# Slot list in bf16 digits, and the lower rows of six output tiles scaled on ScalarE and added by transfers

## The chip, the cores and the metric

One NeuronCore of a Trainium2 chip runs the whole program. The metric is the device time of one execution in microseconds (us). Five engines work beside each other and meet only at semaphores: TensorE (PE in the profile, its weight loads PEld), VectorE (DVE), ScalarE (ACT), GpSimd (POOL) and SyncE (SP, which here only starts transfers). Sixteen DMA engines carry what SP, ACT and POOL put into their queues.

## The reference

1024 tokens of 512 values each. A dense layer with a LoRA adapter for each sequence gives the input of a feed-forward part: a router picks 2 of 16 experts for every token, every expert is a small gated network, and a shared gated network of width 256 is added.

```
xt     = x @ W.T + b + 2 * (x @ A[slot]) @ B[slot]
scores = softmax(xt @ router_w + router_b) + router_bias
idx    = top 2 experts of a token, out of its 2 best groups of 4
y      = sum over experts e of gate[:, e] * ((silu(xt@w1+b1) * (xt@w2+b2)) @ w3 + b3)
z      = (silu(xt@sw1+sb1) * (xt@sw2+sb2)) @ sw3 + sb3
out    = x + y + z
```

## The kernel before

The 1024 tokens are 8 tiles of 128 rows (`TILES`, `P`). The body of each engine is one list of instructions in a written order; waits on semaphores are the only thing that ties the engines together, and whatever stands behind a wait on an engine waits too. Products that need accuracy are written as a sum of three fp32r products of high and low parts (`product`, L1024): ACT makes the high part by a cast, DVE the low part by a subtraction (`rest`, L715).

Stage 1 (to about 46 us): the dense layer and LoRA (`cond_w`, `cond_lora`, `mask_lh`, `hi_lhT`), the transposed tokens (`turn_xt`, `hi_xtT`, `lo_xtT`) and the router (`logits`, `shift_logits`, `exps`, `choose`). Transposed tokens pass through two buffers `xtT_whole`; `hi_xtT(i)` may fill one only after `lo_xtT(i-2)` has read it. POOL makes constants between its LoRA gathers (L433 to L445).

Stage 2 (to about 76 us): PE does the first products of the shared network (`shared_up`), and between them the bookkeeping of the routing. The (token, expert) pairs are sorted by expert into blocks of 128 slots, each block with one expert. DVE works out the position of every pair, `off_i` within a block and `blk_i` the block, and makes the one-hot tables `onehot_off` (L862) and `blk_hit` (L858). POOL multiplies `blk_hit` by the pair's number (L458). Sixteen fp32r matmuls of 32 columns (L1197) turn them into the slot list. From it come `slot_tok` (what POOL gathers), `slot_row` (where results are scattered), `eid` (the expert of each block) and `low_known` (how many blocks must be stored before the final rows may be loaded).

Stage 3 (76 to 131 us): 18 blocks in this execution. For each block POOL gathers 128 token rows (L469), PE turns them (L1207), multiplies by the expert's weights (L1222, L1233), ACT copies weights and tokens to fixed places, DVE multiplies and copies the result, and POOL scatters it to `y_rows` in HBM (L475). PE is one block ahead.

Stage 4 (the tail): each token has two result rows, a lower and an upper one. SP loads the 8 lower tiles in four transfers (`low_in`) and the 8 upper ones in four (`high_in`, L398), the last as soon as the last scatter has landed. PE makes the shared network's output of tile i in a PSUM bank (two `product` calls and one matmul L1297, then `shared_done`). For tiles 5, 6 and 7 (`LOW_ON_PE`) it also adds the lower rows times their weight, by a matmul with a diagonal matrix (L1303). DVE adds to `x_sb`, tile after tile: `add_low` for tiles 0 to 4 (L987), `add_high` (L992), `add_shared` (L984). SP stores each finished tile, one transfer per `acc_done`.

Of the kernel before, what the change touches and what calls it, by code (L numbers as in the profile page):

```python
# [37 lines left out]
LOW_ON_PE = (5, 6, 7)  # L38
# [21 lines left out]
def program(nc, x, xT, seq_slot, condWT, cond_b, lora, router_w, router_b, router_bias,  # L60
# [5 lines left out]
    with ExitStack() as ctx:  # L66
# [32 lines left out]
        def at(kib, name, shape, dt=F32):  # L99
            return nc.alloc_sbuf_tensor_at(name, shape, dt, offset=arena_at + kib * 1024)  # L100
# [8 lines left out]
        diag = at(104, "diag", [P, len(LOW_ON_PE), P])  # L109
# [31 lines left out]
        onehot_off = at(152, "onehot_off", [P, K * TILES, P], F32R)  # L141
        hsT_sb = at(160, "hsT_sb", [P, IC, T])
        hsT_split = at(152, "hsT_h", [P, IC, T], F32R), at(160, "hsT_l", [P, IC, T], F32R)
        blk_tok = at(168, "blk_tok", [P, K * TILES, BPAD], F32R)
        blk_hit = at(172, "blk_hit", [P, K * TILES, BPAD])
# [66 lines left out]
        pair_row = sb("pair_row", [P, K * TILES])  # L212
# [45 lines left out]
        diag_ready = sem("diag_ready")  # L258
# [148 lines left out]
        def _(pool):  # L407
# [21 lines left out]
            def gather_lora(g):  # L429
                if g >= 2:  # L430
# [7 lines left out]
            gather_lora(1)  # L438
            pool.affine_select(out=tmp[:], in_=tmp[:], compare_op=ALU.not_equal, fill=1.0, base=0,
# [16 lines left out]
            by_block = [P, K * TILES, BPAD]  # L456
            pool.wait_ge(blk_hit_ready, 1)
            pool.tensor_tensor(blk_tok[:], blk_hit[:], pair_row[:].unsqueeze(2).to_broadcast(by_block), ALU.mult  # L458
                               ).then_inc(blk_tok_ready, 1)
# [36 lines left out]
            left = blocks_left(pool)  # L496
            for g in range(FULL // UNROLL, LOOP_END // UNROLL + 1):
                with pool.If(top == (g - 1) * UNROLL):
                    for n in range(DRAINED):
                        with pool.If(left > n):  # L500
                            scatter(g * UNROLL + n)


        @block.scalar
        def _(act):
# [58 lines left out]
            for i in range(TILES):  # L564
                g = i // 2 + 1
                if i in (2, 4, 6):
                    copy_lgT((i - 2) // 2)
                if i % 2 == 0 and g < GROUPS_L:
                    hi_lora(g)
                if i in (3, 5, 7):  # L570
                    exps((i - 3) // 2)
                if i % 2 == 1 and g < GROUPS_L:
                    hi_lhT(g)
# [28 lines left out]
            for u in range(3):  # L602
                gate_silu(u)
# [7 lines left out]
            hi_hs(2)  # L611
            act.wait_ge(b3s_in, 16)
            act.copy(b3s_split[:], b3s_raw[:]).then_inc(b3s_hi, 1)
            gate_silu(3)
# [34 lines left out]
            for b in range(2):  # L649
                e = expert_of(b)  # L650
                take_w12(b, b, e)
                take_b12(b, b, e)
# [6 lines left out]
            silu(0, 0)  # L659
            hi_hs(3)  # L660
            top = last_group(act)
            left = blocks_left(act)

# [18 lines left out]

            for n, i in enumerate(LOW_ON_PE):
                act.activation(diag[:, n, :], ident[:], ACT.Copy, scale=val[:, 0, i:i + 1]).then_inc(diag_ready, 1)
# [3 lines left out]
        def _(dve):  # L688
# [106 lines left out]
            then(dve.tensor_scalar(pair_row[:], slot_no[:, 0:K * TILES], float(-K * T), None, ALU.add))  # L795
# [10 lines left out]
            for i in range(TILES):  # L806
                if i % 2 == 0:
                    add_cond(i)
                    add_cond(i + 1)
                if i in (3, 5, 7):  # L810
                    shift_logits((i - 3) // 2)
                if i in (4, 6):
                    choose((i - 4) // 2)
                g = i // 2 + 1
                if i % 2 == 0 and g < GROUPS_L:
                    lo_lora(g)
                if i % 2 == 1 and g < GROUPS_L:
                    mask_lh(g)
                if i % 2 == 0 and g + 2 < XCHUNKS:
                    lo_xT(g + 2)  # L820
                if i >= 1:
# [31 lines left out]
            with nc.allow_low_precision(reason="positions are whole numbers below 2 ** 13"):  # L853
# [5 lines left out]
                              cols_i[:, 0:BPAD].unsqueeze(1).to_broadcast([P, NJ, BPAD]), ALU.is_equal).then_inc(blk_hit_ready, 1)  # L859
            for j in range(0, NJ, NJ // 2):  # L860
# [11 lines left out]
            then(dve.tensor_copy(slot_pair[:], bank[6][:, 0:BPAD]))  # L872
            dve.tensor_scalar(slot_tok[:], slot_pair[:], T - 1, None, ALU.bitwise_and).then_inc(slot_tok_ready, 1)
            dve.wait_ge(gate_ones, 2)
            twice = gate[:, :, 0:64].rearrange("p i (m c) -> p i m c", m=2)[:, :, :, 0:E].bitcast(F32R)
            then(dve.tensor_copy(twice, sc[:].unsqueeze(2).to_broadcast([P, TILES, 2, E])))
            dve.tensor_tensor(gate[:, :, 64:64 + E].bitcast(F32R), sc[:], gate[:, :, 0:E], ALU.subtract).then_inc(gate_ready, 1)
            hidden(2)
# [13 lines left out]
            dve.engine_nop().then_inc(eid_ready, 1)  # L892

            then(dve.tensor_scalar(slot_f32, slot_pair[:], float(K * T), None, ALU.add))
            then(dve.tensor_scalar(slot_empty, slot_pair[:], 0.0, None, ALU.is_equal))
            then(dve.tensor_tensor(slot_empty, slot_empty, slot_no[:], ALU.mult))
# [83 lines left out]
            dve.wait_ge(x_in, 16 * TILES)  # L980

            def add_shared(i):
                dve.wait_ge(shared_done, i + 1)
                dve.tensor_tensor(x_sb[:, i, :], x_sb[:, i, :], shared_bank(i)[:], ALU.add).then_inc(acc_done, 1)  # L984

            def add_low(i):
                then(dve.scalar_tensor_tensor(out=x_sb[:, i, :], in0=low_tiles(first, i), scalar=val[:, 0, i:i + 1],  # L987
                                              in1=x_sb[:, i, :], op0=ALU.mult, op1=ALU.add))

            def add_high(i):  # L990
                dve.wait_ge(high_in[i // 2], 16)
                then(dve.scalar_tensor_tensor(out=x_sb[:, i, :], in0=low_tiles(first, TILES + i), scalar=val[:, 1, i:i + 1],  # L992
                                               in1=x_sb[:, i, :], op0=ALU.mult, op1=ALU.add))

            dve.wait_ge(low_in, 16 * TILES // 2)
            add_low(0)
            add_high(0)
            add_shared(0)
            add_low(1)
            add_high(1)  # L1000
            add_shared(1)
            add_low(2)
            add_high(2)
            add_shared(2)
            add_low(3)
            add_high(3)
            add_shared(3)
            add_low(4)
            add_high(4)
            add_shared(4)  # L1010
            add_high(5)
            add_shared(5)
            add_high(6)
            add_shared(6)
            add_high(7)
            add_shared(7)
# [3 lines left out]
        def _(pe):  # L1020
# [172 lines left out]
            pe.wait_ge(blk_tok_ready, 1)  # L1193
# [61 lines left out]
            for b in range(UNROLL):  # L1255
                steps(b, b)
                if b == 0:
                    top = last_group(pe)
                if b == 1:
                    left = blocks_left(pe)  # L1260
                if b == 2:
                    pe.wait_ge(low_known, 1)
                    first = low_at(pe)
# [27 lines left out]
            for i in range(TILES):  # L1291
                if shared_bank(i) in (bank[5], bank[6]):
                    pe.wait_ge(acc_done, 1)
                for c in range(IC):
                    product(shared_bank(i)[:], [part[:, c, i * P:(i + 1) * P] for part in hsT_split],
                            [part[:, c, :] for part in sw3_split], start=(c == 0), stop=False)
                mm = pe.matmul(shared_bank(i)[:], gateT[:, i * P:(i + 1) * P], b3s_split[:], start=False,  # L1297
                               stop=(i not in LOW_ON_PE))
                if i in LOW_ON_PE:
                    n = LOW_ON_PE.index(i)  # L1300
                    pe.wait_ge(diag_ready, n + 1)
                    pe.wait_ge(low_in, 16 * TILES // 2)
                    mm = pe.matmul(shared_bank(i)[:], diag[:, n, :], low_tiles(first, i), start=False, stop=True)  # L1303
                mm.then_inc(shared_done, 1)
# [49 lines left out]
```

## Time and profile before

| | |
|---|---|
| time, median of 3 runs | 152.35 us (152.08 to 152.58) |
| time of the profiled execution | 152.1 us |
| its span | 150.3 us |
| PE busy | 142.7 us, 95% of the span |
| PEld busy | 112.3 us, 75% |
| DVE busy | 90.9 us, 60% |
| ACT busy | 70.6 us, 47% |
| POOL busy | 53.0 us, 35% |
| moved by DMA | 41.09 MB, 273 GB/s over the span |

The span is what the profile covers; 1.8 us of the execution lie around it. The span in 40 slices, a digit being tenths of a slice in which the engine was busy (DMA: the mean of 16 engines):

```profile
PE   7969999999978999999999999999999999999991
DVE  1683556355997959998853545663333223499992
ACT  3561274366633646018596665566556665300000
DMA  4979999999994999911653356876788999786963
```

A slice is 3.76 us. PE is near 9 throughout; the 7 and 8 of its twelfth and thirteenth slices are at 41 to 49 us. The DMA row is high again in the last quarter, where result rows are scattered, loaded and stored.

### The profile page before, as it was taken

How to read it: one execution, taken by the hardware profiler on the slowest of the kernel's cores; microseconds unless marked ns; L12 is line 12 of the kernel's file. 1: busy time of each engine (PE TensorE's matmuls, PEld its weight loads, DVE VectorE, ACT ScalarE, POOL GpSimd, SP SyncE). 2: the span in 40 equal slices, each digit the busy share in tenths (PEclk: the TensorE clock that was granted, in tenths of full speed). 3: DMA queues.
4: the chain of work that ended last, by engine and by line, in shares of the span. 5: the costliest groups of instructions: out<-in, count | busy, mean ns of one | idle time of the engine just before them, and what ended most of it. 6: DMA issues, size and time to landing. Idle time of an engine off the chain costs nothing.

```text
span 150.3 us, 3119 instructions
## 1 busy us (share of the span) xinstructions
PE 142.7 (95%) x990; PEld 112.3 (75%) x991; DVE 90.9 (60%) x230; ACT 70.6 (47%) x138; POOL 53.0 (35%) x68
## 2 busy tenths in 40 slices
PE   7969999999978999999999999999999999999991
PEld 7747676776755877888898887888778887688760
DVE  1683556355997959998853545663333223499992
ACT  3561274366633646018596665566556665300000
POOL 7570211000000020135542767667575666350000
PEclk9999999999999999999999999999999999999999
DMA  4979999999994999911653356876788999786963
GB/s 143 345 239 336 415 394 404 339 382 413 417 412 158 289 388 369 391 48 39 190 141 125 99 184 190 298 227 246 265 286 236 368 400 324 227 325 197 293 253 140
DMA packets 16767, 41.09 MB, mean 273 GB/s; under 512 B 2448, under 2 KB 2448, under 8 KB 16624
## 3 DMA queue, kind: packets, MB, share of 16 engines
q1 hardware_dynamic: 11488, 23.33, 43.5%
q0 software_dynamic: 3776, 12.59, 25.0%
q10 hardware_dynamic: 1488, 4.98, 9.0%
q8 instruction: 8, 0.13, 0.3%
q14 instruction: 7, 0.06, 0.1%
HBM read 31.98 MB, written 8.91 MB: 272 GB/s over the span
## 4 chain that ended last, share of the span: by engine, by line
PE 77%; DVE 7%; DMA 5%; ACT 3%; issue 3%; POOL 2%; POOLq 0%; DVEq 0%
PE bank L1024 28%; PE bank L1222 21%; PE bank L1233 10%; DMA lora_raw<-in_lora,lora_row 5%; PE bank L1207 5%; PE bank L1080 2%; PE bank L1303 2%; PE bank L1090 2%; DVE xt_ring L746 1%; PE bank L1297 1%; PE bank L1099 1%; PE bank L1197 1%; ACT xtT_h L539 1%; PE bank L1057 1%; DVE xT_l L715 1%
## 5 line engine op out<-in xcount | busy, mean ns | idle before, releaser
L1222 PE MATMUL bank<-xgT_sb,w_now 128*128 128x128 f32 x288 | 35.2, 275 | 0.0
L1222 PEld LDWEIGHTS bank<-xgT_sb,w_now 128*128 128x128 f32 x288 | 33.6, 192 | 0.6 <-issue 0.5
L469 POOL DMA_INDIRECT xg_sb<-xt_rows,slot_tok x22 | 21.4, 971 | 12.7 <-issue 5.5
L475 POOL DMA_INDIRECT y_rows<-y_ring,slot_row x18 | 19.3, 1070 | 15.3 <-DVE y_ring L930 15.0
L922 DVE SCALAR_TENSOR_TENSOR hT_sb<-bank,b_now,glT_sb 128x128 f32<-128x128 f32 x18 | 6.3, 351 | 25.3 <-ACT glT_sb L636 22.7
L626 ACT COPY w_now<-w_sb 128x1024 f32 x18 | 18.9, 1048 | 0.8 <-issue 0.8
L618 ACT COPY xgT_sb<-bank 128x512 f32<-128x512 f32 x18 | 10.5, 585 | 18.5 <-PE bank L1207 18.5
L1233 PE MATMUL bank<-w_sb,hT_sb 128*128 x36 | 18.3, 593 | 0.0
L930 DVE COPY y_ring<-bank 128x512 f32<-128x512 f32 x18 | 12.4, 691 | 6.8 <-PE bank L1233 6.8
L1207 PEld LDWEIGHTS bank<-ident,xg_sb 128*128 128x128 f32 x72 | 8.9, 141 | 8.0 <-issue 7.9
L1024 PE MATMUL bank<-condW_h,xT_h 128*128 128x512 f32 x31 | 13.4, 433 | 1.3 <-DVE xT_l L715 1.2
L1024 PE MATMUL bank<-xtT_h,sw_h 128*128 128x512 f32 x32 | 13.2, 414 | 0.0
L1024 PE MATMUL bank<-xtT_h,sw_l 128*128 128x512 f32 x32 | 12.6, 393 | 0.0
L1024 PE MATMUL bank<-xtT_l,sw_h 128*128 128x512 f32 x32 | 12.5, 391 | 0.0
L1024 PE MATMUL bank<-condW_h,xT_l 128*128 128x512 f32 x31 | 12.2, 393 | 0.0
L1024 PE MATMUL bank<-condW_l,xT_h 128*128 128x512 f32 x31 | 12.1, 391 | 0.0
L452 POOL MEMSET gate<- 128x768 f32 x1 | 0.7, 740 | 32.2 <-PE bank L1110 32.2
L1207 PE MATMUL bank<-ident,xg_sb 128*128 128x128 f32 x72 | 10.8, 272 | 0.0
L1024 PEld LDWEIGHTS bank<-condW_h,xT_h 128*128 128x128 f32 x31 | 5.8, 188 | 3.9 <-DVE xT_l L715 1.6
L433 POOL DMA_INDIRECT lora_raw<-in_lora,lora_row x4 | 4.1, 1037 | 12.5 <-DVE loraB_l L715 10.9
L715 DVE TENSOR_TENSOR xT_l<-xT_raw,xT_h 128x1024 fp32r<-128x1024 f32 (+2 forms) x6 | 5.7, 962 | 3.7 <-ACT xT_h L510 3.7
L636 ACT ACTIVATE glT_sb<-bank,b_now 128x128 f32<-128x128 f32 x18 | 6.7, 372 | 1.7 <-PE bank L1222 1.7
(178 smaller groups left out, 247.2 us busy)
## 6 DMA issues: line engine op xcount, KB each, us to landing
w_sb<-in_w SPq DMA_DIRECT2D x8, 1024.0 KB, 9.6
w_sb<-in_w ACTq DMA_DIRECT2D x2, 2048.0 KB, 13.8
low_sb<-y_rows SPq DMA_DIRECT2D x8, 512.0 KB, 5.8
xt_rows<-xt_ring SPq DMA_DIRECT2D x8, 256.0 KB, 5.4
x_sb<-in_x SPq DMA_DIRECT2D x8, 256.0 KB, 2.9
out<-x_sb SPq DMA_DIRECT2D x8, 256.0 KB, 3.4
xT_raw<-in_xT SPq DMA_DIRECT2D x3, 512.0 KB, 7.0
sw_raw<-in_sw SPq DMA_DIRECT2D x1, 1024.0 KB, 8.7
```

The costliest lines, as they stand in the source:

```text
L469: pool.indirect_dma_start(xg_sb[:, b % 4, :], None, xt_rows, bass.IndirectOffsetOnAxis(ap=slot_tok[:, b:b + 1], axis=0)).then_inc(gathered ...
L475: pool.indirect_dma_start(y_rows, bass.IndirectOffsetOnAxis(ap=slot_row[:, b:b + 1], axis=0), y_place(b), None).then_inc(y_scattered[b % Y ...
L618: act.copy(xgT_sb[:, s % 2], bank[s % 2][:].rearrange("p (k t) -> p k t", k=KC)).then_inc(xgT_copied, 1)
L626: act.copy(w12_now[:, s % 2, :], w12_sb[:, bass.ds(e * W12, W12)]).then_inc(w12_ready, 1)
L636: act.activation(glT_sb[:, s % 2, :], gate_bank(s)[:, 0:P], ACT.Silu, bias=b12_now[:, s % 2, 0:1]).then_inc(act_ready, 1)
L715: dve.tensor_tensor(lo, whole, hi.bitcast(F32), ALU.subtract).then_inc(made_sem, 1)
L922: dve.scalar_tensor_tensor(out=hT_sb[:, s % 2, :], in0=up_bank(s)[:, 0:P], scalar=b12_now[:, s % 2, 1:2], in1=glT_sb[:, s % 2, :], op0=ALU ...
L930: dve.tensor_copy(y_place(s), bank[5 + s % 2][:]).then_inc(y_copied, 1)
L1024: mm = pe.matmul(out, a[p], b[q], start=(start and n == 0), stop=(stop and n == 2))
L1207: mm = pe.transpose(bank[s % 2][:, k * P:(k + 1) * P], xg_sb[:, s % 4, k * P:(k + 1) * P], ident[:])
L1222: mm = pe.matmul(half[:, 0:P], w12_now[:, s % 2, (2 * k + m) * INTER:(2 * k + m + 1) * INTER], xgT_sb[:, s % 2, k, :], start=(k == 0), sto ...
L1233: pe.matmul(bank[5 + s % 2][:], hT_sb[:, s % 2, :], w3_sb[:, bass.ds(e * DIM, DIM)], start=True, stop=True).then_inc(y_done, 1)
```

## The change

1. Slot list. A pair's number is now written as two digits in base 128 (a tile digit and a partition digit) in bf16. DVE makes the first digit's table after `blk_hit` (two-operand product, 128x512), ACT the second (an activation placed between `gate_silu(1)` and `gate_silu(2)`); POOL's product is gone. `onehot_off` and `blk_hit` are bf16, and the 16 matmuls have 64 columns in bf16. DVE puts the digits together with one instruction more.
2. Stage 2 order. DVE makes `eid` right after `slot_tok`, ahead of the gate table and `hidden(2)`. ACT moves `hi_hs(2)` behind `silu(0, 0)` and `gate_silu(3)` between the first two weight copies.
3. Stage 1 order. POOL waits for the last `condW` low part (`condW_done`) before its four constants. In turns 3 and 5 DVE does `mask_lh` ahead of `shift_logits`, and ACT `hi_lhT` ahead of `exps`; `lo_xtT(3)` moves from turn 4 to turn 5. In turn 7 `shift_logits` keeps its place.
4. Tail. `LOW_BY_DMA` is tiles 2 to 7. ACT scales their lower rows in place once all are loaded, POOL adds each to `x_sb` by a transfer that accumulates, behind its last scatter. DVE adds lower rows for tiles 0 and 1 alone. The diagonal matmuls and their ACT tables are gone. POOL and ACT now read `first` from `eid`, after `low_known`.

```diff
-LOW_ON_PE = (5, 6, 7)
+LOW_BY_DMA = range(2, TILES)
 POOL, constants
+            pool.wait_ge(condW_done, KC)
             pool.affine_select(out=tmp[:], ...
 POOL, slot list
-            pool.tensor_tensor(blk_tok[:], blk_hit[:], pair_row[:].unsqueeze(2).to_broadcast(by_block), ALU.mult
-                               ).then_inc(blk_tok_ready, 1)
 POOL, behind the last scatter
+            pool.wait_ge(x_in, 16 * TILES)
+            for n, i in enumerate(LOW_BY_DMA):
+                pool.wait_ge(low_scaled, n + 1)
+                pool.dma_start(x_sb[:, i, :], low_tiles(first, i), accum_op=ALU.add).then_inc(low_added[n], 16)
 ACT
+            act.wait_ge(blk_hit_ready, 1)
+            act.activation(blk_tok[:, :, 1, :], blk_hit[:], ACT.Copy, scale=part_f[:, 0:1]).then_inc(blk_tok_ready, 1)
...
-                act.activation(diag[:, n, :], ident[:], ACT.Copy, scale=val[:, 0, i:i + 1]).then_inc(diag_ready, 1)
+            act.wait_ge(low_in, 16 * TILES // 2)
+            for i in LOW_BY_DMA:
+                act.activation(low_tiles(first, i), low_tiles(first, i), ACT.Copy, scale=val[:, 0, i:i + 1]).then_inc(low_scaled, 1)
 DVE
+            dve.tensor_tensor(blk_tok[:, :, 0, :], blk_hit[:], tile_digit[:].unsqueeze(2).to_broadcast([P, NJ, BPAD]), ALU.mult
+                              ).then_inc(blk_tok_ready, 1)
...
+            then(dve.tensor_scalar(slot_high[:], bank[6][:, 0:BPAD], float(P), None, ALU.mult))
+            then(dve.tensor_tensor(slot_pair[:], slot_high[:], bank[6][:, BPAD:2 * BPAD], ALU.add))
...
 DVE, tail
             add_low(0)
+            add_low(1)
             add_high(0)
             add_high(1)
+            for i in range(TILES):
+                add_shared(i)
+                if i + 2 < TILES:
+                    add_high(i + 2)      (waits for high_in[i // 2] and low_added of its tile)
 PE
-                mm = pe.matmul(bank[6][:, 0:BPAD], onehot_off[:, j, :], blk_tok[:, j, :],
+                mm = pe.matmul(bank[6][:, 0:2 * BPAD], onehot_off[:, j, :], blk_tok[:, j].rearrange("p d b -> p (d b)"),
...
-                if i in LOW_ON_PE:
-                    mm = pe.matmul(shared_bank(i)[:], diag[:, n, :], low_tiles(first, i), start=False, stop=True)
```

## Rows read from the trace of the kernel before

**Rows 1.** Page, section 4: shares of the chain that ended last, by engine.

```profile
PE 77%; DVE 7%; DMA 5%; ACT 3%; issue 3%; POOL 2%; POOLq 0%; DVEq 0%
```

**Rows 2.** Chain in order of time (start us, us, what): first LoRA gather.

```profile
5.49 8.20 DMA lora_raw<-in_lora,lora_row
```

**Rows 3.** Timeline of DVE, 6 to 9 us (start us, us, engine line op).

```profile
6.38 0.69 DVE L715 TENSOR_TENSOR condW_l<-condW_raw,condW_h 128x512 fp32r<-128x512 f32 x1
...
7.97 1.25 DVE L715 TENSOR_TENSOR xT_l<-xT_raw,xT_h 128x512 fp32r<-128x512 f32 x1 [0.91 <-ACT xT_h L510]
```

**Rows 4.** Timelines of DVE and of PE, 37 to 46 us.

```profile
37.40 1.23 DVE L715 TENSOR_TENSOR sw_l<-sw_raw,sw_h 128x1024 fp32r<-128x1024 f32 x1 [1.20 <-ACT sw_h L583]
...
44.64 0.19 DVE L759 TENSOR_TENSOR lgs<-bank,red 128x32 f32<-128x32 f32 x1
...
45.73 0.50 PE L1080 MATMUL bank<-loraB_h,lhT_h 64*128 64x512 f32 x2 [1.42 <-DVE lhT_l L715]
```

**Rows 5.** Slot list: timelines, chain pieces, and line L862 (ns min/median/max).

```profile
62.57 0.69 DVE L858 TENSOR_TENSOR blk_hit<-blk_i,cols_i 128x512 f32<-128x512 int32 x1
63.35 1.96 POOL L458 TENSOR_TENSOR blk_tok<-blk_hit,pair_row 128x512 fp32r<-128x512 f32 x1 [7.10 <-DVE blk_hit L858]
...
64.89 0.69 ACT L594 ACTIVATE sg_sb<-bank,sb_sb 128x512 f32<-128x512 f32 x1 [5.39 <-PE bank L1024]
...
59.04 0.22 PE bank L1186 x7
...
66.21 1.69 PE bank L1197 x16
...
L862 DVE TENSOR_TENSOR onehot_off<-off_i,cols_i x2: 1217/1643/2069, 63.2 to 64.3; 128x1024 fp32r<-128x1024 int32 x2
```

**Rows 6.** Timelines of DVE, ACT and PE, up to the first expert block.

```profile
72.52 0.17 DVE L890 TENSOR_SCALAR eid<-eid_f 1x32 int32<-1x32 f32 x1
...
73.63 1.05 ACT L626 COPY w_now<-w_sb 128x1024 f32 x1 [0.78 <-issue]
...
75.72 0.57 ACT L618 COPY xgT_sb<-bank 128x512 f32<-128x512 f32 x1
...
76.50 0.68 PE L1222 MATMUL bank<-xgT_sb,w_now 128*128 128x128 f32 x4
```

**Rows 7.** Tail: chain pieces, then timeline of DVE.

```profile
141.21 0.86 PE bank L1303 x2
...
147.13 0.69 DVE x_sb L984
```

**Rows 8.** Tail: line L992, last scatter and its landing, last load and its landing.

```profile
L992 DVE SCALAR_TENSOR_TENSOR x_sb<-low_sb,val,x_sb x8: 745/752/753, 132.9 to 146.2; 128x512 f32<-128x512 f32 x8
...
132.93 0.97 POOL L475 DMA_INDIRECT y_rows<-y_ring,slot_row x1 [0.30 <-issue]
...
DMA to landing us min/median/max: 4.5/4.8/5.1
...
137.75 0.37 SPq L398 DMA_DIRECT2D low_sb<-y_rows  x1
...
DMA to landing us min/median/max: 5.2/5.2/5.2
```

**Rows 9.** Stretches: us, busy of PE, PEld, DVE, ACT, POOL, granted clock, DMA share, GB/s.

```profile
120.00:124.00 4.00, 4.00 (x31) 3.43 (x30) 1.04 (x2) 2.79 (x7) 2.67 (x3) 1.00 1.05 397
...
132.00:136.00 4.00, 4.00 (x19) 3.24 (x18) 3.63 (x7) 0.00 (x0) 1.59 (x2) 1.00 0.87 334
136.00:140.00 4.00, 4.00 (x19) 3.27 (x18) 3.68 (x6) 0.00 (x0) 0.00 (x0) 1.00 0.67 182
140.00:144.00 4.00, 4.00 (x18) 2.76 (x16) 3.79 (x6) 0.00 (x0) 0.00 (x0) 1.00 0.96 342
144.00:147.00 3.00, 3.00 (x11) 1.65 (x9) 2.88 (x5) 0.00 (x0) 0.00 (x0) 1.00 0.49 187
147.00:150.30 3.30, 0.03 (x1) 0.00 (x0) 0.69 (x1) 0.00 (x0) 0.00 (x0) 0.97 0.42 159
```

More of the change, by code:

```diff
@@ L257, in program @@
         shared_done = sem("shared_done")
-        diag_ready = sem("diag_ready")
+        low_scaled = sem("low_scaled")
+        low_added = [sem(f"low_added{i}") for i in LOW_BY_DMA]
         low_in = sem("low_in")
@@ L496, in _ @@
             left = blocks_left(pool)
+            pool.wait_ge(low_known, 1)
+            first = low_at(pool)
             for g in range(FULL // UNROLL, LOOP_END // UNROLL + 1):
@@ L600, in hi_hs @@
                 act.copy(hsT_split[0][:, c, n * HALF:(n + 1) * HALF], hsT_sb[:, c, n * HALF:(n + 1) * HALF]).then_inc(hs_hi, 1)
-            for u in range(3):
-                gate_silu(u)
+            gate_silu(0)
+            gate_silu(1)
+            act.wait_ge(blk_hit_ready, 1)
+            act.activation(blk_tok[:, :, 1, :], blk_hit[:], ACT.Copy, scale=part_f[:, 0:1]).then_inc(blk_tok_ready, 1)
+            gate_silu(2)
             act.wait_ge(slots_done, 1)
@@ L648, in _ @@
             act.wait_ge(sh_up_done, IC)
[L649 to L652, printed above, removed]
+            e = expert_of(0)
+            take_w12(0, 0, e)
+            take_b12(0, 0, e)
+            gate_silu(3)
+            e = expert_of(1)
+            take_w12(1, 1, e)
+            take_b12(1, 1, e)
             act.wait_ge(sh_up_done, 2 * IC)
@@ L662, in _ @@
             left = blocks_left(act)
+            act.wait_ge(low_known, 1)
+            first = low_at(act)
             def group(b):
@@ L794, in _ @@
             then(dve.tensor_copy(slot_no[:], slot_no_i[:]))
-            then(dve.tensor_scalar(pair_row[:], slot_no[:, 0:K * TILES], float(-K * T), None, ALU.add))
+            then(dve.tensor_copy(part_f[:], part_i[:]))
+            then(dve.tensor_scalar(tile_digit[:], cols[:, 0:K * TILES], float(TILES), None, ALU.add))
+            then(dve.tensor_scalar(slot_no_pad[:], slot_no[:], float(K * T + T), None, ALU.add))
             lo_lora(0)
@@ L818, in _ @@
                     mask_lh(g)
+                if i in (3, 5):
+                    shift_logits((i - 3) // 2)
+                if i == 5:
+                    lo_xtT(3)
                 if i % 2 == 0 and g + 2 < XCHUNKS:
                     lo_xT(g + 2)
-                if i >= 1:
+                if i >= 1 and i != 4:
                     lo_xtT(i - 1)
@@ L892, in _ @@
             dve.engine_nop().then_inc(eid_ready, 1)
-            then(dve.tensor_scalar(slot_f32, slot_pair[:], float(K * T), None, ALU.add))
+            dve.wait_ge(gate_ones, 2)
+            twice = gate[:, :, 0:64].rearrange("p i (m c) -> p i m c", m=2)[:, :, :, 0:E].bitcast(F32R)
+            then(dve.tensor_copy(twice, sc[:].unsqueeze(2).to_broadcast([P, TILES, 2, E])))
+            dve.tensor_tensor(gate[:, :, 64:64 + E].bitcast(F32R), sc[:], gate[:, :, 0:E], ALU.subtract).then_inc(gate_ready, 1)
+            hidden(2)
+            then(dve.tensor_scalar(slot_f32, slot_pair[:], float(-T), None, ALU.add))
             then(dve.tensor_scalar(slot_empty, slot_pair[:], 0.0, None, ALU.is_equal))
-            then(dve.tensor_tensor(slot_empty, slot_empty, slot_no[:], ALU.mult))
+            then(dve.tensor_tensor(slot_empty, slot_empty, slot_no_pad[:], ALU.mult))
             then(dve.tensor_tensor(slot_row[:], slot_f32, slot_empty, ALU.add))
@@ L980, in _, with add, add_low, add_high @@
             dve.wait_ge(x_in, 16 * TILES)
+            added = {}
+            def add(i, ins):
+                made[0] += 1
+                added[i] = made[0]
+                ins.then_inc(dve_step, 1)
+            def add_low(i):
+                add(i, dve.scalar_tensor_tensor(out=x_sb[:, i, :], in0=low_tiles(first, i), scalar=val[:, 0, i:i + 1],
+                                                in1=x_sb[:, i, :], op0=ALU.mult, op1=ALU.add))
+            def add_high(i):
+                dve.wait_ge(high_in[i // 2], 16)
+                if i in LOW_BY_DMA:
+                    dve.wait_ge(low_added[i - LOW_BY_DMA[0]], 16)
+                else:
+                    dve.wait_ge(dve_step, added[i])
+                add(i, dve.scalar_tensor_tensor(out=x_sb[:, i, :], in0=low_tiles(first, TILES + i), scalar=val[:, 1, i:i + 1],
+                                                in1=x_sb[:, i, :], op0=ALU.mult, op1=ALU.add))
@@ L982, in add_shared @@
             def add_shared(i):
                 dve.wait_ge(shared_done, i + 1)
+                dve.wait_ge(dve_step, added[i])
                 dve.tensor_tensor(x_sb[:, i, :], x_sb[:, i, :], shared_bank(i)[:], ALU.add).then_inc(acc_done, 1)
[L986 to L993, printed above, removed]
@@ L1013, in _ @@
[L1013 to L1016, printed above, removed]
+            for i in range(TILES):
+                add_shared(i)
+                if i + 2 < TILES:
+                    add_high(i + 2)
         @block.tensor
```

60 lines of the change are left out of this document (16 added, 44 removed).

## The prediction, made before the changed kernel was run

> **What bounds the kernel now.** I read the chain that ended last first. Three quarters of it are PE [rows 1], and the page has PE busy for 95% of the span: time is won where PE gets less work or loses a wait, and only if nothing else is late. So I went to the timelines of the four places that the change touches, and last to the stretches of the tail. There PE is not alone. It ends at about 147.1 and DVE's last add follows at once [rows 7], but the DMA engines carry 4.5 MB at the same time and in single stretches are 87 to 96% busy [rows 9]. The span ends 150.3 - 147.13 - 0.69 = 2.5 us behind that add, with the last store.
>
> **Constants behind the condW parts.** DVE's subtraction of 128x512 takes 0.69 us alone and 1.25 us beside POOL's constants [rows 3]. Moving them gives PE up to 0.6 us before 13 us. But PE needs the first LoRA gather next, which lands at 5.49 + 8.20 = 13.69 us [rows 2], and PE had finished by then. I take nothing; between 0 and 0.15.
>
> **Order in stage 1.** PE waits 1.42 us for DVE's `lhT_l` at 45.73 [rows 4]. In turn 5 two things leave the place ahead of it: the logits' shift, two instructions at about 0.2 each [rows 4], and `lo_xtT(3)`, a subtraction of 128x512, 0.69 [rows 3] and about 0.6 without its overlap with the next: 1.0 in all. In turn 3 the same order costs something. ACT's `exps(0)` now waits for a shift that stands behind `lhT_l`, and everything behind it on ACT slides by some 0.6 us: the transposed tokens and the cast for `sw_l`. DVE already waited 1.20 us for that cast, at 37.40 [rows 4], and `add_cond(4)` and all up to `mask_lh(3)` stand behind it. So DVE begins turn 4 0.6 later and PE gets its operand 1.0 - 0.6 = 0.4 us earlier. Bounds: 0 and 1.4, the whole wait. DVE's next add for PE then comes some 0.2 late, which PE's 1.6 us of `shared_up` in between cover.
>
> **Slot list.** The 16 fp32r matmuls are 1.69 us of the chain; 7 bf16 matmuls of up to 112 columns, with the same number of weight columns, are 0.22 [rows 5], 0.03 each. Sixteen make 0.5: 1.2 us less. Is PE's operand there? DVE gets a product of 128x512, priced at `blk_hit`'s 0.69, ahead of the one-hot tables. But one of these takes 1.22 and the other, beside POOL's 1.96 us product, 2.07 [rows 5]. Without POOL both should take the shorter time, 0.85 back. The tables are ready about when they were, some 0.2 behind PE's arrival. ACT's digit lies in a gap of 5.39 us before its next `silu` [rows 5]. One more DVE instruction ahead of `slot_tok` puts the gathers back by 0.2.
>
> What is late next is ACT. PE's first expert matmul is at 76.50, the ACT copy that it needs starts at 75.72, the weight copy before it at 73.63, and that waits for `eid`, made at 72.52 [rows 6]. `eid` now comes ahead of the gate table and `hidden(2)` (1.3 us), and 0.2 later for the extra instruction. But `gate_silu(3)` (0.65) has moved between the two weight copies. The copy of the tokens comes at about 74.9 against 75.72 and PE starts 0.8 us earlier instead of 1.2. Bounds: 0.3 (if the register reads in between are dearer) and 1.2. What ACT has more to do after `silu(0)` is one cast and one register read, perhaps 0.7 us; I leave it uncounted, since ACT is idle for half of the span, and let the lower bound hold it. Sum so far 0.4 + 0.8 = 1.2 us less before the block loop (0.3 to 2.6). The loop is bound by PE in both, and passes the shift on.
>
> **The tail, by PE and DVE.** Three diagonal products of 0.86 [rows 7] leave PE: 2.6 us. PE would be done at 147.1 - 1.2 - 2.6 = 143.3. DVE loses three `add_low` of 0.75 (as L992 [rows 8]) and does 2 low, 8 high and 8 shared adds, some 12 us from 130.8: it has room. If nothing else counted, the last add would end at 144.0, the span at 146.5 and the time at 148.3.
>
> **The tail, by the transfers.** Tiles 2 to 7 now wait for a transfer before `add_high`. POOL issues them behind its last scatter, which takes POOL from 132.93 to 133.90 [rows 8]; 1.2 earlier and a gap of 0.3: first issue at 133.0. Behind POOL's waits stands nothing but the next add. ACT's six scalings (128x512, half of the 1.05 of its weight copy [rows 6], from 128) are over by 131.5. An accumulating transfer is not in this trace. For its issue I take the scatter's 0.97 + 0.3; for the landing the 4.5 of the last scatter [rows 8]. The sixth is issued at 133.0 + 5 x 1.27 = 139.4 and lands at 143.9; then follow `add_high(7)`, `add_shared(6)` and `add_shared(7)`, 1.95 us: 145.8. The upper rows are no later: their last load starts at 137.75, lands 5.2 later [rows 8], and comes 1.2 earlier. With the last store the span would be 148.3.
>
> That holds only if the DMA engines have room. Share times length of the stretches from 132 to 150.3 is 3.5 + 2.7 + 3.8 + 1.5 + 1.4 = 12.9 us of all engines, for 4.5 MB: 351 GB/s [rows 9]; the fullest stretch earlier reached 397 [rows 9]. The six adds move 6 x 0.262 = 1.57 MB. At a copy's price that is 4.5 us more. A copy reads once and writes once; an accumulation reads source and destination and writes: three movements for two, 6.7 us. If reading alone is the limit it is double, 9.0 us. With 12.9 us of work begun at 130.8, and 1 us in which the engines can't be full (one store alone at the end), the span ends at
>
> - copy's price: 130.8 + 12.9 + 4.5 + 1 = 149.2
> - half more: 151.4
> - double: 153.7
>
> I take half more, because it counts every movement that the instruction names, and keep both ends for the range. The work does not fit beside the old traffic: the loads of the upper rows and the stores share the engines with the adds, DVE waits for each add, and the stores, which need DVE, are pushed behind.
>
> The Trainium skill speaks against this part: "Collectives: The Full Stack", section "The bandwidth ceiling: the fold count and why AG ≠ RS ≠ AR", says that a DMA with an add is about half as fast as a copy, since it needs two source reads on the same ring, with a measured ratio of 1.93. By that rule the last line would hold; nothing in this trace shows an add, so it stands as the rival below.
>
> **To the time.** The profiled execution took 152.1 for a span of 150.3, and is 0.25 below the median of the runs. So I add 1.8 + 0.25 to a span: 151.4 gives 153.4 us.
>
> **The rivals.**
> (a) The adds are cheap, or the shares of [rows 9] are waiting rather than work (one stretch reads 1.05), so that they overlap for nothing. Then the chain of issues decides: span 148.3 to 149.2, time 150.3 to 151.2, best guess 150.6: faster. For it: 182 GB/s between 136 and 140. It decides if an add takes less than about 0.9 us of all 16 engines (0.262 MB at 351 GB/s is 0.75).
> (b) Double price: span 153.7, time 155.7. Against it: 397 GB/s in the fullest stretch, which would take 1.5 off.
> (c) The reorderings give nothing (ACT's `exps` eats the first, the register reads the second) and the tail costs what the adds cost at the copy's price: 151.2 + 1.2 = 152.4, no change. Against it: PE's 1.42 us wait is plain.
> (d) PE's floor, 148.3, if POOL's plain transfers take less than the indirect ones and land in 3 us.
>
> **Chances.** Forecast 0.35; (a) 0.31; (b) 0.22; (c) 0.08; (d) 0.04. The range takes in (a) and most of (b): 150.2 to 156.0; the forecast's own is 152.6 to 154.3. About 0.3% can be told from no change. Faster: (a), (d) and a tenth of the rest, 0.38. Same 0.11. Slower 0.51.
>
> **What the profile would show.** PE's wait at 45.7 shrunk to about 1.0 with a new one of up to 0.5 at the turn of tile 4, near 39; the 16 matmuls of L1197's place at 0.5 us in all; the first expert matmul near 75.3; PE's end near 143. For the forecast: DMA share at 0.9 or more from 134 to the end, adds that land 6 us or more after issue, and DVE idle in front of most `add_high`. It is wrong if adds land within 4.5 us at POOL's pace of 1.3 us (a), or if POOL needs 2 us or more for one issue, which no row excludes and which would put the end back by 5 x 0.7 us without any full DMA engine.

## The result, and the profile of the changed kernel

| | before | changed |
|---|---|---|
| median of the runs | 152.47 us (152.08 to 152.67, 4 runs) | 156.12 us (155.54 to 157.71, 4 runs) |
| ratio | 1 | 1.026, 95% interval 1.018 to 1.034 |
| profiled execution / its span | 152.1 / 150.3 us | 156.24 / 154.5 us |
| PE busy | 142.7 us, 95% | 139.0 us, 90% |

The change is slower by 3.65 us, 0.12 above the upper end of the range. PE has 3.7 us less work, and the time went to the DMA engines. Page of the changed kernel: head, the span in 40 slices, queue q0 (packets, MB, share of 16 engines), and the chain's shares by engine:

```profile
span 154.5 us, 3127 instructions
...
PE 139.0 (90%) x984; PEld 109.7 (71%) x985; DVE 88.4 (57%) x231; ACT 74.2 (48%) x142; POOL 57.2 (37%) x73
...
PE   7967999999889999999999999999999999999300
...
DVE  1664556354989969999815645552333234906563
...
DMA  4989999999993999904740558768879996899995
...
q0 software_dynamic: 4640, 14.16, 30.2%
...
PE 59%; DMA 16%; ACT 7%; DVE 6%; issue 5%; ACTq 2%; POOL 2%; DVEq 1%; SPq 0%; POOLq 0%
```

Read the right end. PE's row stops at the digit 3 (its last matmul ends at 144.35 us), DVE's row has a 0 at slice 36 where before it was full, and the DMA row stays at 8 or 9 until the last slice. In the chain DMA rose from 5% to 16% and PE fell from 77% to 59% [rows 1].

The tail in order of time, and what DVE's line of `add_high` waited for (count, busy, ns of one, idle before it):

```profile
132.86 1.34 POOL L475 DMA_INDIRECT y_rows<-y_ring,slot_row  x1 [0.30 <-ACT low_sb L698]
134.20 5.47 POOL L508 DMA_DIRECT2D x_sb<-low_sb  x6
...
138.94 0.75 DVE L1022 SCALAR_TENSOR_TENSOR x_sb<-low_sb,val,x_sb 128x512 f32<-128x512 f32 x1 [3.66 <-DMA x_sb<-low_sb]
...
150.00 0.75 DVE L1022 SCALAR_TENSOR_TENSOR x_sb<-low_sb,val,x_sb 128x512 f32<-128x512 f32 x1 [0.66 <-DMA x_sb<-low_sb]
150.67 1.28 DVE L1028 TENSOR_TENSOR x_sb<-x_sb,bank 128x512 f32<-128x512 f32 x2
...
DMA to landing us min/median/max: 4.5/8.9/12.8
...
L1022 DVE SCALAR_TENSOR_TENSOR x_sb<-low_sb,val,x_sb 128x512 f32<-128x512 f32 x8 | 5.9, 750 | 8.0 <-DMA x_sb<-low_sb 8.0
```

The scatter that took 0.97 us in [rows 8] takes 1.34. POOL then starts six adds between 134.2 and 137.0, 0.56 us apart. The first lands 4.5 us behind its issue, the last 12.8, so they land 2.0 to 2.7 us apart, from 138.7 to 149.8. DVE waits 8.0 us in all for them, and ends at 151.95. The last add of before ended at 147.82 [rows 7].

The stretches of the tail, with the columns of [rows 9]:

```profile
136.00:140.00 4.00, 4.00 (x19) 3.28 (x18) 1.06 (x2) 0.00 (x0) 3.67 (x5) 1.00 1.04 225
140.00:144.00 4.00, 4.00 (x19) 3.21 (x18) 1.95 (x4) 0.00 (x0) 0.00 (x0) 1.00 1.09 262
144.00:148.00 4.00, 0.35 (x2) 0.00 (x0) 2.38 (x5) 0.00 (x0) 0.00 (x0) 0.79 1.10 262
```

Here is the loss. The engines are full (1.04 to 1.10; a share a little above 1 is read as full) and carry 225 to 262 GB/s. Before, a share of 1.05 carried 397 [rows 9]. So the bytes that the profile counts are not all the work that an add is.

Ahead of the block loop, the marks of the changed kernel:

```profile
5.39 9.08 DMA lora_raw<-in_lora,lora_row
...
40.62 0.66 PE L1112 MATMUL bank<-ident,xt_ring 128*128 128x128 f32 x4 [0.65 <-DVE xt_ring L760]
...
46.15 0.50 PE L1102 MATMUL bank<-loraB_h,lhT_h 64*128 64x512 f32 x2 [0.50 <-DVE lhT_l L729]
...
66.66 0.51 PE bank L1219 x16
...
76.02 2.02 PE L1244 MATMUL bank<-xgT_sb,w_now 128*128 128x128 f32 x16
...
80.06 0.59 ACT L626 COPY xgT_sb<-bank 128x512 f32<-128x512 f32 x1 [1.28 <-issue]
```

The first gather lands at 14.47 us, not 13.69 [rows 2], 0.8 later. PE's wait for `lhT_l` has gone from 1.42 [rows 4] to 0.50, and 0.65 of it is back as a wait at the turn of tile 4: the matmuls are 0.42 us later than before where the gather was 0.78 later, so the order gained 0.36. The sixteen slot matmuls take 0.51 us for 1.69 [rows 5]. The first expert matmul is at 76.02 against 76.50 [rows 6].

### The profile page after: what moved, and what is told of

It reads as the page before. It is cut to its first block, busy times and chain, and to the rows that moved or that the text cites. A ratio compares the mean times of both kernels' runs of the same rounds, so it can differ in the third digit from the quotient of the medians.

```text
span 154.5 us, 3127 instructions
## 1 busy us (share of the span) xinstructions
PE 139.0 (90%) x984; PEld 109.7 (71%) x985; DVE 88.4 (57%) x231; ACT 74.2 (48%) x142; POOL 57.2 (37%) x73
## 3 DMA queue, kind: packets, MB, share of 16 engines
q1 hardware_dynamic: 11488, 23.33, 42.9%
q0 software_dynamic: 4640, 14.16, 30.2%
## 4 chain that ended last, share of the span: by engine, by line
PE 59%; DMA 16%; ACT 7%; DVE 6%; issue 5%; ACTq 2%; POOL 2%; DVEq 1%; SPq 0%; POOLq 0%
PE bank L1046 20%; PE bank L1244 18%; PE bank L1255 8%; DMA x_sb<-low_sb 8%; DMA lora_raw<-in_lora,lora_row 6%; PE bank L1229 5%; DMA slot_i<-in_seq_slot 2%; PE bank L1102 2%; ACT low_sb L698 2%; PE bank L1112 1%; POOL x_sb L508 1%; DVE xt_ring L760 1%; PE bank L1121 1%; PE bank L1079 1%; DVE xT_l L729 1%
## 5 line engine op out<-in xcount | busy, mean ns | idle before, releaser
L1022 DVE SCALAR_TENSOR_TENSOR x_sb<-low_sb,val,x_sb 128x512 f32<-128x512 f32 x8 | 5.9, 750 | 8.0 <-DMA x_sb<-low_sb 8.0
L729 DVE TENSOR_TENSOR xT_l<-xT_raw,xT_h 128x1024 fp32r<-128x1024 f32 (+2 forms) x6 | 5.1, 868 | 4.9 <-ACT xT_h L517 4.9
```

The lines of the kernel that those rows point to most:

```text
L729: dve.tensor_tensor(lo, whole, hi.bitcast(F32), ALU.subtract).then_inc(made_sem, 1)
L1022: add(i, dve.scalar_tensor_tensor(out=x_sb[:, i, :], in0=low_tiles(first, TILES + i), scalar=val[:, 1, i:i + 1], in1=x_sb[:, i, :], op0=AL ...
```

## The experiments

Each ran beside the kernel before on the same chip. Times are medians, and ratios are to that kernel.

### The halves of the change

a1: the changed kernel with the old tail. a2: the kernel before with the new tail.

```diff
a1, from the changed kernel          a2, from the kernel before
-LOW_BY_DMA = range(2, TILES)        -LOW_ON_PE = (5, 6, 7)
+LOW_ON_PE = (5, 6, 7)               +LOW_BY_DMA = range(2, TILES)
(and all lines of the diff's part 4 that go with it)
```

> The changed kernel with the tail of the kernel before: diagonal products on PE for tiles 5 to 7, low adds of tiles 0 to 4 on DVE, no accumulating transfer. Theory (the tail's adds cost all of the loss): the block loop starts as in the profile of after, at most 0.1 us ahead of before, and the time is 0 to 0.3 us under before. Rival (the loss sits ahead of the loop, hidden by the tail): 1 us or more over before. If the late first LoRA gather (14.47 against 13.69 us) is chance of one execution, the time is 0.8 us under before.

> The kernel before with nothing changed but the tail: six lower rows scaled by ACT and added by accumulating transfers. Theory: the tail alone costs what the whole change cost, 3.5 to 4.5 us over before. ACT's extra wait and register read after its first silu should show as a later second or third block, up to 0.3 us. Rival: the tail costs 2 us or less and the rest comes from the other edits.

a1: 151.31 (10 runs) against 152.29, ratio 0.995 (0.991 to 0.998). a2: 156.87 (4 runs) against 152.29, ratio 1.029 (1.022 to 1.037). So the head gives 1.0 us (0.3 to 1.4) and the tail costs 4.6 (3.3 to 5.6), and 4.6 - 1.0 = 3.6, for 3.65 measured. The tail is the whole loss. That the two add up to within 0.1 us is partly luck: their intervals are wider, and ACT's wait and register read ahead of the block loop, which costs the changed kernel 0.4 us (b3 below), is in neither number. a1 leaves it out, and in a2 the fourth block comes 26.41 us behind the first counting matmul, against 26.36 before.

### What an add costs: copies in their place

a3 leaves the addition out: the six transfers overwrite `x_sb`, so x is missing from tiles 2 to 7. Same bytes, same order, same waits.

```diff
-                pool.dma_start(x_sb[:, i, :], low_tiles(first, i), accum_op=ALU.add).then_inc(low_added[n], 16)
+                pool.dma_start(x_sb[:, i, :], low_tiles(first, i)).then_inc(low_added[n], 16)
```

> As the changed kernel, but the six transfers copy the scaled lower rows over x instead of adding them, so x is left out of tiles 2 to 7. Same queue, size, place and waits. Theory (an add costs the 16 engines twice a copy, because it reads source and destination): the software queue's share falls by 4.5 us of all engines, the copies land 1.0 to 1.3 us apart instead of 2.0 to 2.7, the last one lands near 143 instead of 149.8, and the time falls by 3 us or more, to about 152 to 153. Rival (the queue behind the scatters, or descriptor building on POOL, is slow whatever the operation): landings and time stay within 0.5 us of the changed kernel.

152.91 us (one run, before 152.29), 3.2 less than with adds, or 3.0 if each is set against the kernel before beside it. Two lines of queues before; then a3's line of q0, its six issues on POOL's timeline and their landings, and two of its stretches:

```profile
q1 hardware_dynamic: 11488, 23.33, 43.5%
q0 software_dynamic: 3776, 12.59, 25.0%
```

```profile
q0 software_dynamic: 4256, 14.16, 27.8%
...
134.50 3.27 POOL L508 DMA_DIRECT2D x_sb<-low_sb  x6
...
DMA to landing us min/median/max: 3.4/6.4/7.4
...
136.00:140.00 4.00, 4.00 (x19) 3.28 (x18) 1.35 (x2) 0.00 (x0) 1.77 (x4) 1.00 0.96 321
140.00:144.00 4.00, 4.00 (x19) 3.25 (x18) 2.45 (x4) 0.00 (x0) 0.00 (x0) 1.00 1.03 377
```

Set q0's share times span side by side: before 25.0% of 150.3 = 37.6 us of all engines; with copies 27.8% of 151.2 = 42.0; with adds 30.2% of 154.5 = 46.7. Six copies are 4.4 us, six adds 9.1. The prediction's two ends were 4.5 and 9.0. Each of the two is good to about 1 us only: q0's share times span is 37.3 to 38.6 us in the profiles of a1, b4, c1, c2, c3 and c4, which have none of these transfers. The difference of 4.7 between adds and copies does not hang on that (it is 5.6 between b1 and b2 below).

The line of q0 counts 12.59 MB before and 14.16 in both others, 1.57 more for adds as for copies. So an add costs more time for the same counted bytes: full engines show 377 GB/s here and 262 there. That this is the second read is the likely reading, but no run shows it by itself. For the lines of q0 differ in one thing more: six copies are 480 packets, six adds 864, 1.8 times as many, so an add is also made in more and smaller pieces. Small packets alone are a weak rival: q1's have 2.03 KB on average, and 23.33 MB in 43.5% of 150.3 us of all engines is 357 GB/s.

### The same, with nothing else on the engines

b1 and b2 make POOL wait for all loads of the upper rows, and hold the stores back until all six transfers have landed. b2 has copies, and leaves x out as a3 does.

```diff
+            for n in range(len(LOW_BY_DMA)):
+                sp.wait_ge(low_added[n], 16)          (SP, ahead of the stores)
...
+            for n in range(TILES // 2):
+                pool.wait_ge(high_in[n], 16)          (POOL, ahead of the six)
```

> The changed kernel with its six adds put where nothing else is on the DMA engines: POOL waits for all upper rows first, SP stores nothing before the sixth add has landed. It measures the price of an add by itself; the time is of no interest and will be some us longer. Theory (an add is twice a copy): after the first landing, adds land 1.3 to 1.5 us apart (twice 0.262 MB at 397 GB/s), and the stretch reads about 190 GB/s at a full DMA share. Rival (an add is slow only for the company of loads and stores): 0.7 to 0.9 us apart.

> As the kernel with the adds alone, but six plain copies over x, so x is left out of tiles 2 to 7. Theory: they land 0.65 to 0.75 us apart, half of the adds. Rival (POOL's issues, 0.56 us apart, or the queue set the pace of both): the same spacing as the adds.

b1's adds land at 146.1 to 153.3, 1.44 us apart; b2's copies at 144.7 to 148.7, 0.80 apart. The issues (the last starts at 145.4 in b1 and at 145.2 in b2), the landings and the stretch from 146 to 148, first of b1, then of b2:

```profile
142.62 5.44 POOL L512 DMA_DIRECT2D x_sb<-low_sb  x6 [8.41 <-DMA low_sb<-y_rows]
...
DMA to landing us min/median/max: 3.5/5.8/7.9
...
146.00:148.00 2.00, 0.00 (x0) 0.00 (x0) 1.47 (x3) 0.00 (x0) 2.00 (x3) 0.97 1.09 182
```

```profile
142.40 3.34 POOL L512 DMA_DIRECT2D x_sb<-low_sb  x6 [7.83 <-DMA low_sb<-y_rows]
...
DMA to landing us min/median/max: 2.3/3.1/3.5
...
146.00:148.00 2.00, 0.00 (x0) 0.00 (x0) 2.00 (x4) 0.00 (x0) 0.00 (x0) 1.00 0.98 363
```

Alone, full engines carry half the counted bytes with adds (182 for 363 GB/s). 1.44 / 0.80 = 1.8, and the queue's time above gave 9.1 / 4.4 = 2.07. POOL is busy longer with an add than with a copy (5.44 us for six, 3.34 for six), but 0.91 us for each is less than the 1.44 between landings: the full engines set the pace, not POOL. The Trainium skill gives a measured ratio of 1.93 in "Collectives: The Full Stack", section "The bandwidth ceiling: the fold count and why AG ≠ RS ≠ AR", for traffic between cores made of copies against the same with adds. It lies between these two.

### Fewer adds

a4 has adds for tiles 5 to 7 alone; DVE does the lower rows of tiles 0 to 4 ahead of the first upper rows. PE is as unburdened as in the changed kernel.

```diff
-LOW_BY_DMA = range(2, TILES)
+LOW_BY_DMA = range(5, TILES)
...
-            add_low(0)
-            add_low(1)
+            for i in range(5):
+                add_low(i)
```

> As the changed kernel, but only tiles 5, 6 and 7 are added by transfers; DVE adds the lower rows of tiles 0 to 4 first. Theory (each add takes 2 to 2.7 us one behind the other from 134.2): the three land by about 143.5, when DVE has just the last upper rows to add; the last add ends near 145.7, the span near 148.3, and the time is 1.5 to 2.5 us under before. Rival (the loss is a fixed one, the first wait of 3.7 us and crowded stores, whatever the number): time within 1 us of the changed kernel.

151.8 us (10 runs) against 152.29, ratio 0.997 (0.993 to 1.000): a miss. It takes 2.6 us from PE and gains nothing on a1. The three adds were in place by 143.9. DVE waited for something else, on its timeline of a4:

```profile
140.50 0.75 DVE L1022 SCALAR_TENSOR_TENSOR x_sb<-low_sb,val,x_sb 128x512 f32<-128x512 f32 x1 [1.02 <-DMA low_sb<-y_rows]
...
144.47 0.75 DVE L1022 SCALAR_TENSOR_TENSOR x_sb<-low_sb,val,x_sb 128x512 f32<-128x512 f32 x1 [1.36 <-DMA low_sb<-y_rows]
```

The wait is not for an add but for the plain loads of the upper rows. The last was issued at 137.1 and landed 7.2 us later, at 144.3, where before it was 137.75 + 5.2 = 142.9 [rows 8]. The adds share the engines with this load and put it back. So do copies: in a3 it took 7.6 us.

### Adds by an engine that is idle

b4 gives the three adds to POOL itself, as two-operand additions in SBUF. ACT's wait for `low_known` is moved behind the loop too, as in b3.

```diff
-                pool.dma_start(x_sb[:, i, :], low_tiles(first, i), accum_op=ALU.add).then_inc(low_added[n], 16)
+                pool.tensor_tensor(x_sb[:, i, :], x_sb[:, i, :], low_tiles(first, i), ALU.add).then_inc(low_added[n], 1)
```

> The changed kernel, with ACT's read late, and tiles 5, 6 and 7 added by POOL itself: one tensor add of 128x512 in SBUF for each, no transfer; DVE adds the lower rows of tiles 0 to 4 first. If the engines' double work was the trouble, the upper rows are no longer late: DVE ends near 144.8 instead of 147.67 with three adds by transfer, and the time is 2 us or more under before, near 150. Against it: POOL's product of the same size took 1.96 us beside a DVE instruction with two operands in SBUF, which took 0.85 longer; if the two hinder each other here, POOL takes 2 us for each add and DVE loses up to 2.5 us, and the time is at that of before.

152.7 us (10 runs) against 152.62, ratio 1.000 (0.996 to 1.004). The loads are on time again (the last took 4.1 us), but another resource is shared. Timelines of DVE and of POOL in b4:

```profile
130.91 7.30 DVE L1013 SCALAR_TENSOR_TENSOR x_sb<-low_sb,val,x_sb 128x512 f32<-128x512 f32 x5
...
133.19 3.80 POOL L508 TENSOR_TENSOR x_sb<-x_sb,low_sb 128x512 f32<-128x512 f32 x3
```

DVE's same five in a4:

```profile
131.64 3.39 DVE L1013 SCALAR_TENSOR_TENSOR x_sb<-low_sb,val,x_sb 128x512 f32<-128x512 f32 x5
```

DVE loses 7.30 - 3.39 = 3.9 us, as much as POOL's three take (3.80). They did not run beside one another but in turns, and DVE was then late to the end. The Trainium skill has this in "SBUF — State Buffer", section "🔬 SBUF: two separate sides": DVE with two SBUF inputs and a GpSimd operation that reads SBUF take one pair of ports in turns, each for its whole instruction. The two rows agree.

### The head, part by part

b3 is the changed kernel with ACT's wait for `low_known` and its register read moved from ahead of the block loop to behind it.

```diff
-            act.wait_ge(low_known, 1)
-            first = low_at(act)
...
+            act.wait_ge(low_known, 1)
+            first = low_at(act)
             act.wait_ge(low_in, 16 * TILES // 2)
```

> The changed kernel with ACT's wait for low_known and its register read moved from its first silu to behind the block loop. Theory (this wait and read hold back the copies for the third block, which PE waits for): the first expert matmul of the fourth block, as counted from the first counting matmul, comes 0.4 us earlier (25.4 instead of 25.8), and the time falls by 0.4 us. Rival (the two casts moved there are the cause): less than 0.15 us.

155.14 us (4 runs) against 152.62, ratio 1.016 (1.009 to 1.024), 1 us less than the changed kernel, but the two intervals overlap, so the gain is read from the traces. From the counting matmuls (first at 58.77, 59.22 and 58.70 in before, changed and b3) to the fourth block (85.13, 85.06, 84.14) it is 26.36, 25.84 and 25.44 us. The slot list and the early `eid` gained 0.5, and 0.9 without ACT's read. In the changed kernel that read is part of the `[1.28 <-issue]` above, which is 0.79 in b3, and PE's third block waited for a copy behind it.

c4 is the kernel before with the slot list in digits alone.

```diff
-        blk_tok = at(168, "blk_tok", [P, K * TILES, BPAD], F32R)
+        blk_tok = at(168, "blk_tok", [P, K * TILES, 2, BPAD], BF16)
(with POOL's product made by DVE and ACT, as in the diff's part 1)
```

> The kernel before with nothing but the slot list in bf16 digits: POOL's product gone, DVE's and ACT's digit tables, 16 matmuls of 64 columns in bf16. Theory: the matmuls take 0.5 instead of 1.7 us, but eid is no earlier (0.2 us later), so the first expert matmul waits for ACT, and of the 1.2 us only 0.1 to 0.4 reaches it; the time falls by 0.1 to 0.4 us. Rival (all of it reaches the end): 1.2 us less.

152.7 us (10 runs) against 152.36, ratio 1.001 (0.998 to 1.005). PE and ACT in c4:

```profile
74.59 1.05 ACT L627 COPY w_now<-w_sb 128x1024 f32 x1 [1.66 <-DVEq L899]
...
77.46 2.02 PE L1229 MATMUL bank<-xgT_sb,w_now 128*128 128x128 f32 x16 [0.83 <-issue]
```

The matmuls are 1.2 us shorter, and PE stands 0.83 us in front of the first expert matmul: ACT's weight copy waits for `eid`. From the first counting matmul it is 17.6 us to it, against 17.9 before. In this trace the digits are worth 0.3 alone, which the runs are too few to show, and pay only together with the early `eid`.

### A better version

c1: head of the changed kernel, two tiles by diagonal on PE, six by DVE, each `add_low` placed three tiles ahead so that no addition follows the one whose result it needs. c2: c1 with ACT's `exps` of turns 3 and 5 behind `hi_xtT` and the cast for `sw_h`. c3: c1 without POOL's wait for `condW_done`.

```diff
c1
-LOW_BY_DMA = range(2, TILES)
+LOW_ON_PE = (6, 7)
...
                 add_shared(i)
+                if i + 3 < TILES and i + 3 not in LOW_ON_PE:
+                    add_low(i + 3)
c2
-                if i in (3, 5, 7):
-                    exps((i - 3) // 2)
+                if i == 7:
+                    exps(2)
                 hi_xtT(i)
...
+                if i in (3, 5):
+                    exps((i - 3) // 2)
c3
-            pool.wait_ge(condW_done, KC)
```

> The changed kernel's first three stages with no accumulating transfer: diagonal products on PE for tiles 6 and 7 alone, the other six lower adds on DVE, in an order in which no add follows directly on the one that it needs (as the changed kernel has it for tiles 0 and 1). DVE's adds cost 0.66 each in that order against 0.75 to 0.91 behind one another. Theory (the tail is a balance of PE and DVE as long as the DMA engines are let alone): DVE does 6 + 8 + 8 adds in 14 us from 130.7, PE ends near 144.8, the span near 148.0, and the time is 1.3 to 1.8% under before, 1 us under the kernel with the old tail. Rival (the upper rows, landing near 141.6, and the stores bound it): within 0.3 us of the kernel with the old tail.

> The kernel with two tiles on PE and one edit more: ACT makes the exponentials of turns 3 and 5 behind the transposed tokens and the weight cast instead of ahead of them. Theory (0.6 us of the order's gain in stage 1 is lost because ACT waits there for a shift that now comes late): PE's wait for xt_ring near 40 us (0.65 in the profile of after) goes, lhT_l comes 0.5 us earlier, and the time falls by 0.3 to 0.6 us. Rival (what follows on DVE takes it back): no change.

> The kernel with two tiles on PE, but POOL makes its four constants at once, as before. Theory (nothing of this edit reaches the end, because PE waits for the first LoRA gather anyway): DVE's subtraction takes 1.25 instead of 0.69 us, and the time is the same within 0.3 us. Rival (the later constants let the weight loads start 0.5 us sooner, which holds back the gather, by 0.8 us in the profile of after): 0.3 to 0.8 us faster than with the wait.

| | runs | median | ratio (95%) |
|---|---|---|---|
| c1 | 6 | 150.75 | 0.989 (0.984 to 0.994) |
| c2 | 6 | 149.29 | 0.979 (0.975 to 0.982) |
| c3 | 4 | 150.40 | 0.986 (0.981 to 0.991) |

The kernel before ran at 152.36. c2 beats both kernels. c1 was expected at 1.3 to 1.8% under the kernel before and came to 1.1%; its interval overlaps a1's, so the new tail order is not shown to gain. c2 was expected 0.3 to 0.6 us under c1, and the medians differ by 1.5. Three of c1's six runs had a mean granted clock of 0.989 or less; the other three have a median of 150.34, still 1.05 above c2. The traces show 0.7 of it: c2's first gather landed as late as c3's (14.22 and 14.21 us), so the two can be laid side by side. PE at the turn of tile 4 and at `lhT_l`, first in c3, then in c2:

```profile
40.36 0.66 PE L1101 MATMUL bank<-ident,xt_ring 128*128 128x128 f32 x4 [0.65 <-DVE xt_ring L749]
...
45.88 0.50 PE L1091 MATMUL bank<-loraB_h,lhT_h 64*128 64x512 f32 x2 [0.49 <-DVE lhT_l L718]
```

```profile
39.60 0.60 PE L1104 MATMUL bank<-ident,xt_ring 128*128 128x128 f32 x4
...
45.17 0.50 PE L1094 MATMUL bank<-loraB_h,lhT_h 64*128 64x512 f32 x2 [0.61 <-DVE lhT_l L721]
```

The wait of 0.65 is gone, and 0.71 arrives at `lhT_l` and 0.7 at the last add. c1 and c3 don't differ by more than their intervals, so no effect of POOL's wait is shown. In c3 DVE's `xT_l` took 0.85 beside POOL's constants (0.69 with the wait), and PE stood idle for the gather anyway.

## Why the prediction came out as it did

- **The direction and the mechanism held.** The work does not fit beside the old traffic: the DMA share is 1.04 to 1.10 from 136 to 148, DVE waits in front of six `add_high`, and the adds land 4.5 to 12.8 us after issue.
- **The term that was mis-sized is the price of an add.** The sum took 6.7 us of all engines for six, three movements for a copy's two. The queue's own time shows 9.1, and the transfers alone 1.8 times a copy. That is rival (b), double price, whose 155.7 us is 0.4 below the 156.12 measured. I chose half more because it counts the movements that the instruction names, which makes a read as dear as a write. What was measured is as if the reads alone set the pace, which fits the price but was not tested apart from the number of packets. Against (b) I set the 397 GB/s of the fullest stretch; the three full stretches with adds show 225 to 262, so that objection fell: full engines do not carry 397 GB/s when adds are among the transfers.
- **The other end, a copy's price, was right for a copy:** 4.4 us measured for 4.5, within the 1 us above. But a3's span was 151.2 where that line of the sum gave 149.2. Of the 2.0, 1.03 is its first gather (14.72 for 13.69) and 0.4 is ACT's read (below); 0.6 stays open.
- **POOL's issue was priced too high:** 0.56 us apart for adds and 0.54 for copies, not 1.27. It didn't matter: the first add was issued at 134.2 instead of 133.0, and from there the DMA engines set the pace. ACT's scalings were priced too low: 0.71 us each for 0.52, done at 132.8 and not at 131.5, still ahead of the first add.
- **The gain of 1.2 ahead of the loop** was 1.0 by the runs of a1, which has no read by ACT, and did not show in the profiled execution, whose first gather was 0.8 later. By parts: order in stage 1 -0.36 for the predicted -0.4, with a new wait of 0.65 where one of up to 0.5 was announced, and an old one of 0.50 where 1.0 was. Slot list and expert start -0.9 for -0.8 (16.96 us from the first counting matmul to the first expert matmul, against 17.89). But ACT's wait and register read, which I left uncounted because ACT is idle half the time, cost 0.4 at the third block: a share of busy time over the span says nothing about the ten microseconds in which ACT feeds PE.
- **The sum, with both terms mended:** the fourth block is 0.07 earlier than before instead of 1.2, so the tail's transfers begin at 131.9 and not at 130.8. 131.9 + 12.9 + 9.1 + 1 = 154.9, for a span of 154.5. The form of the sum (begin, work of all engines, 1 us not full) was good to 0.4, which is inside the 1 us to which the 9.1 is known; two of its inputs were not. The range fell short because its upper end took (b) with hardly anything for a late head.
- **Rival (a),** with its 182 GB/s between 136 and 140 as free room, fell: that room would have held copies (a3 moved 321 and 377 GB/s from 136 to 144) but not adds, which take 1.5 us of all engines each where (a) needed under 0.9. **Rival (c)** fell: the head gives 1.0, and adds are not at a copy's price. It was right in one part, as ACT's register read did eat 0.4 of it. **Rival (d)** asked for landings in 3 us; none came below 4.5.
- **Two slips in the numbers.** The chance of "faster" adds up to 0.42 ((a), (d) and a tenth of the other 0.65), not 0.38. And PE's floor of 148.3 adds only 1.8 to the span of 146.5, without the 0.25 that the other times have: 148.55. Neither moves the forecast.

## What to carry to other kernels

An add made by a transfer was paid here as about two copies (1.8 to 2.07) on the DMA engines, and that is not seen in the counted bytes: work out the free share of the engines in the stretch, not the free GB/s, and ask which other loads stand in the same queues. Taking work off the bounding engine gains only if what replaces it (here 2.6 us of matmuls for 9 us of all DMA engines) has room there. A wait or a register read placed ahead of a loop is priced by who stands behind it in the next ten microseconds, not by how idle its engine is over the span.

## What the runs showed of the hardware

- Accumulating transfers of 128 rows of 2 KB within SBUF: 1.44 us apart with nothing beside them, copies 0.80. POOL starts either every 0.54 to 0.56 us, but its record of an add lasts 1.0 to 2.6 us, of a copy 0.54 to 0.60. Six adds are 864 packets and six copies 480, with the same bytes.
- DVE with two operands in SBUF and POOL with two operands in SBUF took turns: 3.39 us became 7.30 beside 3.80 of POOL's. POOL's last scatter took 0.97 in before and a1, and 1.34 in the changed kernel, a4, b4 and c2, in which DVE runs two such operations back to back beside it. That these belong together was not tested.
- The first gather landed at 13.53 (a1) to 14.80 us (b2) in kernels that are equal up to there, so a difference of that size in one trace is not the edit's.
- TensorE's granted clock fell to near half early in some executions. c1's profiled execution is one. Its stretch from 9 to 13 us:

```profile
9.00:11.00 2.00, 1.90 (x5) 1.57 (x6) 1.37 (x4) 1.40 (x2) 0.60 (x3) 0.61 0.52 94
11.00:13.00 2.00, 2.00 (x6) 1.52 (x6) 1.90 (x5) 0.00 (x0) 1.71 (x2) 0.53 0.92 332
```

The granted clock is 0.61 and 0.53 there, the lower of its two levels (1.2 for 2.4 GHz) for most of it, after a stretch from 7 to 9 us in which PE was busy for 0.96 of 2 us. In c3 that stretch had 1.40 us and the clock stayed at 1.00, but in the profiled execution of before it was 0.96 too and the clock stayed up, so this does not settle what makes it fall. PE started 10 matmuls in these 4 us, where c3's started 16 and then waited for the gather. It came to the first gathered rows at 14.91 instead of 14.35 and was 0.55 us behind c3 at `lhT_l` (46.43 to 45.88).

Over the runs of c4 the price is plainer: five at a mean clock of 0.985 to 0.989 took 153.1 to 154.5 us, five at 0.998 or more took 151.9 to 152.3. That is most of c4's spread, and the reason why its median of 152.7 says less than its trace: those five runs at 0.998 or more have a median of 151.98, and the kernel before, beside them, 152.32 in its twelve. In the changed kernel the clock of the last stretches fell too, but behind PE's last matmul, at no cost.
